# Two pairs of projections as 64-row tiles side by side, and four residual tiles in the FFN, in a gated cross-attention block

## What is computed

```python
q = rope(layernorm(x) @ Wq); k, v = split(ctx @ Wkv); k = rope(k)      # 32 heads of 16
attn = softmax(q k^T / 4) v                                            # per head, 256 x 256
x1 = x + tanh(g_xattn) * (attn @ Wout + bout)
h  = layernorm(x1)
y  = relu(h @ up)**2 @ down + (h @ expert) * (sum of the top 2 of h @ gate)
out = x1 + tanh(g_ffn) * (layernorm(y) * gamma + beta)
```

## Time and profile before

| | us |
|---|---|
| median of 3 runs | 1567.08 (1567.04 to 1567.78) |
| the profiled execution | 1566.75 |
| its span | 1564.9 |
| TensorE busy in the span | 1515.9 (97%) |
| weight loads busy | 1125.0 (72%) |
| VectorE busy | 980.2 (63%) |
| ScalarE busy | 635.0 (41%) |
| GpSimd busy | 337.9 (22%) |

### The profile page before, as it was taken

The page is one execution under the profiler, slowest core; times in us unless marked ns, Lnnn a source line. Parts: engine busy times, 40 slices in busy tenths (PEclk is TensorE's granted clock), DMA queues, the critical chain, the costliest instruction groups (busy, mean ns, idle before and its releaser), DMA issues.

```text
span 1564.9 us, 25920 instructions
## 1 busy us (share of the span) xinstructions
PE 1515.9 (97%) x9498; PEld 1125.0 (72%) x9498; DVE 980.2 (63%) x1416; ACT 635.0 (41%) x962; POOL 337.9 (22%) x406
## 2 busy tenths in 40 slices
PE   7789999999999999979999999999999999999997
PEld 6556666666666666646787888878888888788886
DVE  7788888888888888755655436435354264453524
ACT  4365665655555666665432222222222222222221
POOL 5323233333333333112101002001020020110202
PEclk9699999999999999999999999999999999999999
DMA  6645555555555555544411001101011010010101
GB/s 174 142 98 141 134 137 138 131 142 139 135 135 143 127 127 136 121 134 120 147 61 35 27 21 47 35 15 47 21 35 47 1 54 27 22 40 21 55 0 41
DMA packets 80623, 131.11 MB, mean 84 GB/s; under 512 B 21624, under 2 KB 35064, under 8 KB 80504
## 3 DMA queue, kind: packets, MB, share of 16 engines
q1 hardware_dynamic: 80504, 129.48, 32.4%
HBM read 51.17 MB, written 16.78 MB: 43 GB/s over the span
## 4 chain that ended last, share of the span: by engine, by line
PE 88%; DVE 7%; issue 2%; POOL 1%; ACT 1%; DMA 0%; SPq 0%; POOLq 0%; DVEq 0%; ACTq 0%
PE pP L1113 17%; PE pT L1113 11%; PE pA L1314 11%; PE pO L1113 11%; PE pB L1314 11%; PE pA L1211 7%; PE pO L1239 7%; PE pB L1227 3%; PE pM L1113 3%; DVE mneg L1534 3%; PE pP L1120 2%; PE pM L1120 2%; PE pT L1195 1%; PE pM L1281 1%; PE pM L1187 1%
## 5 line engine op out<-in xcount | busy, mean ns | idle before, releaser
L1534 DVE TENSOR_REDUCE mneg<-pA 128x4 f32<-128x1024 f32 x250 | 305.7, 1223 | 97.7 <-PE pA L1211 93.2
L1012 ACT ACTIVATE probs<-pB 128x1024 f32<-128x1024 f32 x249 | 255.8, 1027 | 213.2 <-PE pB L1227 203.3
L811 POOL TENSOR_SCALAR var_eps<-meanvar 128x1 f32<-128x1 f32 x96 | 34.6, 360 | 986.1 <-DVE meanvar L1416 985.9
L1637 DVE TENSOR_TENSOR relu<-relu 128x512 f32<-128x512 f32 x128 | 88.4, 690 | 252.3 <-ACT hid L1066 252.3
L1314 PE MATMUL pA<-dn,hid 128*128 128x512 f32 x768 | 197.1, 392 | 1.7 <-DVE hid L1639 1.5
L1314 PE MATMUL pB<-dn,hid 128*128 128x512 f32 x768 | 195.0, 389 | 0.0
L1113 PE MATMUL pP<-fT,up 128*128 128x512 f32 x768 | 188.5, 394 | 0.0
L1113 PE MATMUL pO<-fT,up 128*128 128x512 f32 x768 | 184.7, 389 | 0.0
L1314 PEld LDWEIGHTS pA<-dn,hid 128*128 128x128 f32 x768 | 142.9, 188 | 34.4 <-DVE hid L1639 5.1
L1113 PEld LDWEIGHTS pO<-fT,up 128*128 128x128 f32 x768 | 144.0, 188 | 30.3 <-issue 0.4
L1314 PEld LDWEIGHTS pB<-dn,hid 128*128 128x128 f32 x768 | 144.1, 188 | 30.0
(11 more groups left out here) (200 smaller groups left out, 1989.8 us busy)
## 6 DMA issues: line engine op xcount, KB each, us to landing
stk<-kT SPq DMA_DIRECT2D x180, 128.0 KB, 2.9
stq<-qT SPq DMA_DIRECT2D x180, 128.0 KB, 2.9
fres<-x_scratch SPq DMA_DIRECT2D x34, 256.0 KB, 2.9
xin<-x SPq DMA_DIRECT2D x32, 256.0 KB, 2.9
numer<-av_s SPq DMA_DIRECT2D x128, 64.0 KB, 2.4
xres<-x SPq DMA_DIRECT2D x32, 256.0 KB, 2.9
x_scratch<-xres SPq DMA_DIRECT2D x32, 256.0 KB, 2.4
out<-y_s SPq DMA_DIRECT2D x32, 256.0 KB, 2.0
```

The lines of the kernel that those rows point to most:

```text
L811: nc.gpsimd.tensor_scalar_add(var_eps[:], meanvar[:, 1:2], EPS).then_inc(ve_made, 1)
L1012: nc.scalar.activation(probs[:, s % 4, :, :, :].rearrange("p a b s -> p a (b s)"), psum[:, :, :], ACT.Exp).then_inc(exp_done, 1)
L1534: nc.vector.tensor_reduce(mneg[par][:, :, 2 * u:2 * u + 2].rearrange("p t q -> p q t"), psum[:, :, :].rearrange("p q (t k) -> p q t k", t= ...
L1637: nc.vector.tensor_tensor(r[:], r[:], r[:], ALU.mult).then_inc(sq_made, 1)
```

## The change

The order of the attention is changed in three ways. K1 with Q1's first half (step 7) and V0 with O1's first half (now step 13) become pairs: each of the 6 matmuls of either is cut into two of 64 rows, and the upper rows of the one run beside the lower rows of the other. That is a first pass of 12 matmuls; in a second pass the halves are swapped, with a wait until the first pass has ended (`rows_done`). The first pass stands between `logits_a` and `logits_b` of the step, the second behind `logits_b`. V0 moves from step 14 to step 13, from bank pP to pM; m0 moves from step 12 to step 11. Before the first pass TensorE waits that the job before K1 or V0 and the job before Q1 or O1 in their banks have been taken out. VectorE's, ScalarE's and GpSimd's code for the attention is the same, and follows the schedule.

In the FFN there are four residual tiles instead of two. SyncE loads all four at once, and then stores the four results; GpSimd adds beta to tile u ahead of the reciprocal root for tile u as before, and behind the last block it adds beta to all four ahead of the four roots.

```diff
@@ SCHEDULE, BANK
-    11: ("O0",),
-    12: ("m0", "qT1"),
-    13: ("O1<",),
-    14: ("V0",),
+    11: ("O0", "m0"),
+    12: ("qT1",),
+    13: ("O1<", "V0"),
+    14: (),
     15: ("O1",),
...
-    "X0": "P", "Q0": "P", "X1": "P", "Q1": "P", "qT0": "P", "qT1": "P", "V0": "P",
-    "K0": "M", "m1": "M", "V1": "T", "kT0": "M", "K1": "M", "kT1": "M", "m0": "M",
+    "X0": "P", "Q0": "P", "X1": "P", "Q1": "P", "qT0": "P", "qT1": "P",
+    "K0": "M", "m1": "M", "V1": "T", "kT0": "M", "K1": "M", "kT1": "M", "m0": "M", "V0": "M",
...
+PAIRS = {7: ("K1", "Q1<"), 13: ("V0", "O1<")}
@@ TensorE
+            def paired(names, i, s, par, swapped):
+                if swapped:
+                    pe.wait_ge(rows_done, pair_number(i, s))
+                sides = []
+                for k, name in enumerate(names):
+                    half, name = (0, name[:-1]) if name[-1] == "<" else (None, name)
+                    b, at, bank = i + LAG[name], (par + LAG[name]) % 2, BANK[name]
+                    if not swapped:
+                        if some(number(name, b) - 1):
+                            pe.wait_ge(taken[bank], number(name, b) - 1)
+                        inputs_of(name, b, half)
+                    rows = slice(HALF_ROWS, P) if (k == 1) != swapped else slice(0, HALF_ROWS)
+                    sides.append(({"P": pP, "M": pM, "T": pT}[bank], rows, half, bank) + factors(name, b, at))
+                for c in range(CC):
+                    for a, w in PASSES:
...
+                        for psum, rows, half, bank, lhs, rhs, _ in sides:
+                            last = nc.tensor.matmul(psum[:, :], lhs(a, c)[rows, :], rhs(w, c)[rows, :],
+                                                    start=opens, stop=closes and half is None)
...
+                if not swapped:
+                    last.then_inc(rows_done, 1)
...
+                    pair = pair_at(i, s)
+                    if pair:
+                        paired(pair, i, s, par, False)
                     if within(i):
                         logits_b(i, par % 2, s)
...
+                    if pair:
+                        paired(pair, i, s, par, True)
                     for name in names_at(i, s):
-                        job(name, i, par)
+                        if name not in pair:
+                            job(name, i, par)
@@ SyncE, FFN
                     for u in range(UT):
-                        n = (j - 1) * UT + u
-                        if u >= 2:
-                            sp.wait_ge(out_made, n - 1)
-                            alone(sp)
-                            sp.dma_start(out_d[n - 2], y_s[:, u - 2, :]).then_inc(out_out[u - 2], INC)
-                        sp.dma_start(fres[u % 2][:], x1_d[n]).then_inc(fres_in[u % 2], INC)
-                    for u in range(UT - 2, UT):
+                        sp.dma_start(fres[u][:], x1_d[(j - 1) * UT + u]).then_inc(fres_in[u], INC)
+                    for u in range(UT):
                         n = (j - 1) * UT + u
                         sp.wait_ge(out_made, n + 1)
@@ GpSimd, FFN, behind the last block
             for u in range(UT):
-                for_output(NB - 1, u, 2 * UT * NB - UT + u + 1)
+                add_beta(NB - 1, u)
+            for u in range(UT):
+                ffn_inv_std(2 * UT * NB - UT + u + 1)
```

More of the change, by code:

```diff
@@ L141, in first_maxima, with pair_at, pair_number @@
     return isinstance(b, int) and b == 0 and u < STEPS - DELAY
+def pair_at(i, s):
+    names = PAIRS.get(s, ()) if within(i) else ()
+    return names if all(live(x.rstrip("<"), i) for x in names) else ()
+def pair_number(i, s):
+    return sum(bool(pair_at(j, t)) for j in range(i + 1) for t in PAIRS if (j, t) <= (i, s))
 def before(names, i):
@@ L154, in number @@
     names = [x for x in ORDER[BANK[name]] if not two_step or x in TWO_STEP]
+    if isinstance(i, int) and i == -1:
+        names.sort(key=lambda x: x[0] != "V")
     return before(names, i) + sum(live(x, i) for x in names[:names.index(name) + 1])
@@ L341, in flamingo_gated @@
         gt_raw = sb2("gt_raw", [P, KC, NEXP])
+        fres += [sb2(f"fres{k}", [P, D]) for k in range(2, UT)]
         second.close()
@@ L359, in flamingo_gated @@
         f_lo = sem("f_lo")
+        rows_done = sem("rows_done")
         o_done = sem("o_done")
@@ L433, in flamingo_gated @@
         z_made = sem("z_made")
-        fres_in = [sem(f"fres_in{k}") for k in range(2)]
+        fres_in = [sem(f"fres_in{k}") for k in range(UT)]
         fres_made = sem("fres_made")
@@ L896, in ffn_inv_std, with add_beta @@
                 inv_std(NT + count)
[L898 to L903, removed]
+            def add_beta(j, u):
+                pool.wait_ge(fres_in[u], INC * (j + 1))
+                nc.gpsimd.tensor_tensor(fres[u][:], fres[u][:], g_beta[:], ALU.add).then_inc(fres_made, 1)
             pool.wait_ge(gb_made, 2)
@@ L910, in fblock @@
                     for u in range(UT):
-                        for_output(j - 1, u, done + u + 1)
+                        add_beta(j - 1, u)
+                        ffn_inv_std(done + u + 1)
                 if not last:
@@ L1160, in opening, with inputs_of, factors @@
                 pe.wait_ge(o_taken, len(OPENING))
+            def inputs_of(name, b, half):
+                if name[0] == "K":
+                    pe.wait_ge(ctx_split, 2 * b + 2)
+                elif name[0] == "O":
+                    pe.wait_ge(at_lo, 2 * b + (1 if half == 0 else 2))
+            def factors(name, b, par):
+                cut = slice(int(name[-1]) * P, (int(name[-1]) + 1) * P)
+                if name[0] == "Q":
+                    return lambda a, c: xnT[a][:, c, :], lambda w, c: wq_s[w][:, c, :], KC
+                if name[0] == "O":
+                    return (lambda a, c: rest(b, c // 2)[:, c % 2, cut] if a else aT_hi[:, c, cut],
+                            lambda w, c: wo_s[w][:, c, :], KC)
+                weights = wk_s if name[0] == "K" else wv_s
+                return (lambda a, c: ctx_s[par][a][:, c, cut], lambda w, c: weights[w][:, c, :], CC)
@@ new lines, in paired @@
+            def paired(names, i, s, par, swapped):
[13 more added lines that the diff above has]
+                    for a, w in PASSES:
+                        opens = not swapped and c == 0 and (a, w) == PASSES[0]
+                        closes = swapped and c == CC - 1 and (a, w) == PASSES[-1]
+                        for psum, rows, half, bank, lhs, rhs, _ in sides:
+                            last = nc.tensor.matmul(psum[:, :], lhs(a, c)[rows, :], rhs(w, c)[rows, :],
+                                                    start=opens, stop=closes and half is None)
+                            if closes and half is None:
+                                last.then_inc(done[bank], 1)
+                if not swapped:
+                    last.then_inc(rows_done, 1)
@@ L1166, in compute @@
                     last = turn(psum, lambda c: xn[:, c * P:(c + 1) * P])
[L1167 to L1179, removed]
+                elif name[0] in "QKVO":
+                    inputs_of(name, b, half)
+                    last = product(psum, *factors(name, b, par), half)
                 elif name[0] in "qk":
@@ L1609, in sum_y, with centre_y @@
                     nc.vector.tensor_tensor(y_s[:, u, :], acc[u], y_s[:, u, :], ALU.add).then_inc(y_made, 1)
-            def norm_y(j, u, count):
+            def centre_y(j, u, count):
                 n = UT * j + u
@@ L1619, in norm_y @@
                                                ALU.mult).then_inc(z_made, 1)
+            def norm_y(j, u, count):
+                n = UT * j + u
+                y = y_s[:, u, :]
+                centre_y(j, u, count)
                 dve.wait_ge(z_made, n + 1)
@@ L1622, in norm_y @@
                 dve.wait_ge(fres_made, n + 1)
-                nc.vector.scalar_tensor_tensor(y, y, rstd[:, 0:1], fres[u % 2][:], ALU.mult,
+                nc.vector.scalar_tensor_tensor(y, y, rstd[:, 0:1], fres[u][:], ALU.mult,
                                                ALU.add).then_inc(out_made, 1)
```

## The result

| | before | after |
|---|---|---|
| median of the runs side by side | 1567.06 (1566.80 to 1567.78) | 1597.37 (1593.05 to 1599.68) |
| the profiled execution, its span | 1566.75, 1564.9 | 1598.04, 1595.9 |
| period of iterations 1 to 12 | 42.06 to 42.09, one of 42.22 | 43.75 to 43.80 |
| iteration 0 | 39.53 | 43.16 |
| first routing matmul of the FFN at | 728.02 | 752.72 |

The changed kernel is slower: ratio 1.0189, 95% interval 1.0167 to 1.0212. The span is 31.0 us longer. Up to the first routing matmul of the FFN it is 24.7; the tail gives 2.85 back; the other 9.1 lie in the blocks of the FFN, where the prediction had put nothing.

What follows compares the result with a forecast made beforehand. TensorE, busy 41.91 of 42.06 us a period, was taken as the bound, also in the FFN until the tail. 1566.75 + 23.1 (attention) - 2.85 (tail) = 1587.0, forecast 1587 us, range 1570 to 1600.

Steps and rivals of the forecast that it cites:

- The period: Attention, iterations 1 to 12: each period longer by +0.68 + 1.61 - 0.53 = +1.76 us, +21.1 in all.
- Step 7: K1 with Q1's first half: first pass waits for VectorE, second for the first; step 8 0.78 late, net +0.68 us.
- the wait on X1's subtraction: Ahead of step 7's first pass: TensorE, ready at 415.81, starts at 416.66 after VectorE's subtraction, a wait of 0.85 us.
- a slot: Two 64-row matmuls of 512 columns side by side on TensorE: taken as 0.225 us, between 0.213 and 0.24.
- From step 9 to step 14, m0 included: Attention, steps 11 to 14: step 13's pair waits for m0's subtraction, +1.39, with m0's transposes 0.22, together +1.61 us.
- That chain: VectorE's gapless work from step 14 to step 1's first logits, 6.74 us long: only -0.53 of some 1.7 comes back.
- What the tiles could gain: Attention, counted on TensorE alone: about 0.8 us gained each period, with step 7 going from 3.61 to 3.4.
- the rival of a VectorE that isn't late: Attention and tail: banks free when the passes come, about 0.8 us less in some 13 periods, 1554 us; chance 0.10.
- the step that costed its V0 move at nothing: Attention, iteration 0: only step 7's pair was counted, +1.4 us for iterations 0 and 13 together.
- the rival in which the clock falls: Attention: TensorE's waits lower its clock, some 3.5 us once a period, 42 more in all, 1629 us; chance 0.04.
- The blocks of the FFN: FFN before its tail: GpSimd's order stays and TensorE doesn't wait, so no change, 0.
- The tail: End of the FFN: sums made earlier no longer run into VectorE's last steps, 0.75 instead of 1.72 us; -2.85 us.

Runs made afterwards that it cites:

- The last run: Changed kernel with part of VectorE's attention work left out, including the reciprocal of step 14: period 41.73 to 41.78 us, total 1567.42 us.

## Why the prediction was right, and where it was not

*The period: right, step by step.* The forecast had +1.76 and it is +1.71. Step 7: +0.68 forecast, and step 9 starts 0.75 later; the wait on X1's subtraction 0.85 forecast, 0.78 measured; a slot 0.225 against 0.23. Step 11: m0 brings 0.22, as forecast. From step 9 to step 14, m0 included, +1.57 (0.75 to 2.32) against +1.61; the first pass follows m0's subtraction, as said, though only some 0.2 us late. From step 14 to step 1 it is -0.62 against -0.53 (7.14 in place of 7.76, 452.69 to 459.83 and 434.68 to 442.44). That chain was right in its price, with one detail off: TensorE's idle time is 0.80 us and not 1.1, ahead of step 0's logits alone, so that it could have been 1.4 earlier at step 1 and not 1.7.

*What the tiles could gain: too high.* The forecast counted 0.8 us a period on TensorE alone, and step 7 without a wait at 3.4. The 0.8 doesn't follow from its own terms: those add to 0.98 (0.39 + 0.39 + 0.20), and a step 7 of 3.4 in place of 3.61 is 0.21 less and not 0.39. The last run shows 0.30, and step 7 at 3.70 (415.18 to 418.88), 0.09 more than before. There each pass takes 1.46 to 1.49 where 1.35 for six slots was set against it: the first slot of each pass costs its cold weights, 0.33 against 0.23, twice in a step. The forecast put these two terms under what the change adds, and left them out of what it could gain; so the rival of a VectorE that isn't late (1554) was too fast as well.

*Iteration 0: the step that costed its V0 move at nothing failed.* The forecast had +0.7 there, for step 7's pair; measured is +3.63. Step 15 of this iteration has no O1 yet, so that TensorE waited for the maxima at the step 0 behind it before the change too. TensorE's timeline there, in the kernel before and in the one after:

```profile
103.35 0.50 PE L1211 MATMUL pA<-stk,stq 48*128 48x256 f32 x4 [1.13 <-DVE mneg L1534]
```

```profile
104.42 0.80 PE L1258 MATMUL pA<-stk,stq 48*128 48x256 f32 x4 [2.33 <-DVE mneg L1587]
```

And a window over what follows in the kernel after (columns as in the earlier trace rows); in the kernel before the granted clock of the same stretch is 1.00:

```profile
104.00:114.00 10.00, 9.58 (x68) 5.95 (x69) 6.13 (x7) 4.24 (x6) 1.27 (x1) 0.66 0.61 132
```

V0 at step 14 was the work that lay beside VectorE's chain. Taken away, it comes back as a wait of 2.33 us, and after that the clock is at its lower level, 1.2 GHz, for part of the next microseconds. Three runs have this wait at about the same length (2.33 to 2.37) and differ in what the clock did then (windows 104 to 114): with step 13's pair alone the granted clock was 0.83 and the iteration took 40.98, in the whole change 0.66 and 43.16, with the moves alone 0.52 and 43.59. The first and the last of the three do the same work in this iteration. With step 7's pair alone, and V0 at its old place, the wait is 1.14 and the iteration 40.32. So the rival in which the clock falls did happen, though once in the attention, and not once a period. Iterations 1 to 12, 13 and 14 came out a little below their terms (20.25 in place of 21.1, and some 0.6 in place of 1.3), and the opening took 0.26 more, so that the attention has +24.7 against +23.1.

*The blocks of the FFN: "nothing" failed.* This is the largest miss, 8.9 us at the trip ends. The step that failed is "Within the blocks the order of GpSimd stays, and TensorE doesn't wait: nothing": it looked at what the engines wait for from each other, and not at the loop as code. Shown is that the place of the loop in TensorE's program decides, and that TensorE waits there for the second packet of instructions behind the branch. The Trainium skill (Runtime: NRT & Kernel Launch, "Instruction fetch mechanics") says that instructions come in blocks of 256, and that a taken branch to a block outside the current window of two has to fetch it before execution goes on. The traces agree: each branch taken lasts 3.3 to 4.0 us, in the kernel before too, with a packet coming in meanwhile; there it is hidden, since TensorE still has matmuls to do. At which instruction of its block the trip begins is not shown; that it is near the block's end in the programs with the wait is read from the times alone.

*The tail: right.* -2.85, as forecast, with four last steps of 0.75. The Trainium skill's rule on the port that VectorE and GpSimd share (SBUF — State Buffer, "Who interferes with whom") shows in both places: the step of 1.72 is 0.75 without a sum beside it, and beside the four sums in a run the squares take 1.67 in place of 0.69. TensorE waited for none of that (from that block's first routing matmul to TensorE's last matmul it is 97.82 us, and 97.86 before), so the 1.2 that the rule might have cost was rightly left out of the sum.

*The whole.* 1587 was forecast and 1597.4 measured. With the loop moved to a place without the waits it is 1588.8; the 1.8 that are left are the 2.9 of iteration 0 less what the other iterations fell short. That 1597.4 lies within 1570 to 1600 is luck, and owes nothing to the reasons given for that range: its width was for slots and cold weights, which came out close to their terms, and not for the two steps that failed.

## What to carry to other kernels

A period in which one engine is busy for 41.91 of 42.06 us can still be lengthened by nothing but order: ask of each moved instruction when its inputs are ready on the next engine, and what lay beside that engine's chain until now. Price a cover in the first and last iterations too, where other jobs are missing and the cover was the only one. And when a loop follows code that grows, count the instructions ahead of it: a wait of some microseconds at each trip end can come from that alone.

## What the hardware showed that was not expected

- The branch that goes back in a loop holds up TensorE's sequencer for 3.3 to 4.0 us in every program here. TensorE itself waits at such a trip end for nothing or 2.4 to 3.1 us, by the place of the loop in the program; with the lower clock after it each end costs 4.1 to 4.8 us (106.95 and 107.78 against 102.82 and 103.03).
- Semaphore increments on TensorE cost about 0.15 us each at the beginning (23.6 us for 160), and nothing to be seen where the engine waits anyway (period 43.78 with seven of them, 43.77 without).
- Normalising a quarter of the columns saved little where GpSimd's subtraction ran beside it: 1.03 us for 128 columns, ending at 441.57, right after GpSimd's 441.49. In the whole change 512 columns took 1.23 at that place, and the shortest of these steps, 0.55. The length of the step there seems to be set by the other engine.
- After waits of about the same length, 2.33 to 2.37 us, the granted clock of the next microseconds was not the same from run to run: 0.83, 0.66 and 0.52 over the same stretch.
